# Edge stage of a graph attention layer: one exp into a PSUM bank, and the candidates' transposes moved ahead of the residual product

## What is computed

```python
h = (xn @ W).reshape(N, HEADS, HEAD_DIM)
a_src = jnp.einsum('nhd,hd->nh', h, att_src)
a_dst = jnp.einsum('nhd,hd->nh', h, att_dst)
e = jax.nn.leaky_relu(a_src[src] + a_dst[dst], NEG_SLOPE)
emax = jax.ops.segment_max(e, dst, num_segments=N)
ee = jnp.exp(e - emax[dst])
denom = jax.ops.segment_sum(ee, dst, num_segments=N)
agg = jax.ops.segment_sum(h[src] * (ee / denom[dst])[:, :, None], dst, num_segments=N)
out = agg.reshape(N, HEADS * HEAD_DIM) + xn @ W_res + bias
```

## Time and profile before

| | |
|---|---|
| median of 3 runs | 2565.8 us (2564.5 to 2571.7) |
| profiled execution | 2562.1 us |
| its span | 2560.9 us |
| TensorE busy, matmuls | 2062.0 us, 81% |
| VectorE busy | 1652.6 us, 65% |
| ScalarE busy | 1444.0 us, 56% |
| GpSimd busy | 1269.8 us, 50% |

### The profile page before, as it was taken

How to read it: one execution, slowest core, us unless ns; L and a number is a source line. 1 busy time by engine, 2 the same in 40 slices (tenths; PEclk the granted TensorE clock), 3 DMA queues, 4 the chain that set the end, 5 groups by cost and what they waited for, 6 DMA issues and landing times.

```text
span 2560.9 us, 51166 instructions
## 1 busy us (share of the span) xinstructions
PE 2062.0 (81%) x16814; PEld 1778.1 (69%) x16814; DVE 1652.6 (65%) x5168; ACT 1444.0 (56%) x3269; POOL 1269.8 (50%) x1155
## 2 busy tenths in 40 slices
PE   4637777777777777777776999997599999998995
PEld 3525555655555555555665888886599999998995
DVE  4518888888888888888997666664344444443442
ACT  2345555555555555555654666664456656565662
POOL 2167777777777777777740233333123223222221
PEclk8757777777877777777778999997799999999997
DMA  5565555655665565555542222211655254446534
GB/s 139 180 168 167 167 168 173 172 171 171 177 184 173 171 175 170 173 168 173 167 155 85 64 88 84 71 68 54 220 174 165 53 174 102 118 116 230 169 57 117
DMA packets 212241, 369.19 MB, mean 144 GB/s; under 512 B 43768, under 2 KB 147284, under 8 KB 203016
## 3 DMA queue, kind: packets, MB, share of 16 engines
q1 hardware_dynamic: 147560, 213.22, 24.6%
q0 software_dynamic: 63840, 151.61, 24.4%
q10 hardware_dynamic: 576, 1.09, 0.1%
HBM read 438.04 MB, written 101.93 MB: 211 GB/s over the span
## 4 chain that ended last, share of the span: by engine, by line
PE 54%; issue 12%; DVE 12%; ACT 10%; DMA 6%; POOL 3%; SPq 1%; DVEq 1%; ACTq 0%; POOLq 0%
PE bank L917 13%; PE bank L1082 8%; PE bank L1083 8%; PE bank L1084 8%; DVE edge_mem L983 4%; DMA expert_mem<-expert_rows 4%; PE bank L788 3%; ACT edge_mem L818 3%; PE bank L890 3%; PE bank L789 2%; PE bank L906 2%; DVE win_mem L1009 2%; DMA edge_mem<-in_x 1%; ACT piece_hi L710 1%; POOL expert_rows L1259 1%
## 5 line engine op out<-in xcount | busy, mean ns | idle before, releaser
L728 POOL DMA_INDIRECT edge_mem<-node_table,src_col x880 | 912.6, 1037 | 283.5 <-issue 265.2
L917 PE MATMUL bank<-edge_mem 128*128 128x264 f32 x1760 | 536.3, 467 | 15.7 <-DVE win_mem L1009 11.1
L1082 PE MATMUL bank<-expert_rounded 128*128 128x256 f32 x1792 | 517.2, 289 | 0.0
L1083 PE MATMUL bank<-expert_rounded 128*128 128x256 f32 x1792 | 512.4, 286 | 0.0
L1084 PE MATMUL bank<-expert_rounded 128*128 128x256 f32 x1792 | 512.2, 286 | 0.0
L917 PEld LDWEIGHTS bank<-edge_mem 128*128 128x128 f32 x1760 | 397.3, 234 | 133.2 <-issue 50.0
L1783 POOL DMA_INDIRECT sums<-expert_mem,slot_tok x112 | 190.0, 1697 | 546.1 <-DVE expert_mem L1721 459.7
L1770 ACT ACTIVATE expert_mem<-bank,par 128x256 f32<-128x256 f32 x448 | 228.6, 510 | 265.3 <-PE bank L1084 265.1
L1078 DVE TENSOR_TENSOR expert_rounded<-expert_mem,expert_rounded 128x512 fp32r<-128x512 f32 x280 | 193.9, 693 | 283.9 <-ACT expert_rounded L1770 218.5
L1082 PEld LDWEIGHTS bank<-expert_rounded 128*128 128x128 f32 x1792 | 349.9, 195 | 0.0
L1083 PEld LDWEIGHTS bank<-expert_rounded 128*128 128x128 f32 x1792 | 349.4, 195 | 0.0
(11 more groups left out here) (236 smaller groups left out, 3927.0 us busy)
## 6 DMA issues: line engine op xcount, KB each, us to landing
expert_rounded<-split_w SPq DMA_DIRECT2D x224, 1024.0 KB
split_w<-piece_hi SPq DMA_DIRECT2D x72, 256.0 KB
split_w<-piece_lo SPq DMA_DIRECT2D x72, 256.0 KB
piece_full<-in_L_ffn_W SPq DMA_DIRECT2D x64, 256.0 KB
expert_mem<-expert_rows SPq DMA_DIRECT2D x56, 265.0 KB, 3.5
edge_mem<-node_table,src_col POOLq DMA_INDIRECT x880
node_table<-win_mem SPq DMA_DIRECT2D x12, 544.0 KB, 3.8
xn_in<-turned SPq DMA_DIRECT2D x49, 128.0 KB
```

What stands on the lines that cost most here:

```text
L728: pool.indirect_dma_start(gath[g % NGB][:, t, :], None, node_table, bass.IndirectOffsetOnAxis(ap=src_col[:, k, t % 2:t % 2 + 1], axis=0)). ...
L917: ins = pe.matmul(bank[5 + at % 3][:, 0:AGG], onehot[g % 2][:, 2 * k + j, :], gath[g % NGB][:, 2 * k + j, 0:AGG], start=(j == 0), stop=(j ...
L1082: pe.matmul(out_ap, s_hi, m_lo, start=start, stop=False)
L1083: pe.matmul(out_ap, s_lo, m_hi, start=False, stop=False)
```

## The change

One SBUF tile `exponent` holds the scores of 16 tiles and, behind them, the factors' arguments of 8 steps. One exp turns both into a PSUM bank of its own (bank 2), from which `wgt` and `scale` are read; the exp of the factors alone and its semaphore go. The exp waits for the arguments, the scores, the messages and the adds of the round before. The maxima share bank 1 with the edge values, and the maxima's matmuls wait for the scores to be read. On TensorE the candidates' transposes come ahead of the residual product, on ScalarE the residual's copy comes behind the exp and the candidates' middle part.

```diff
--- before.py
+++ after.py
@@ -187,9 +187,8 @@
         rest = sb1("rest", [P, GS, 2 * HEADS])
         shift0 = sb1("shift0", [P, GS, HEADS])
         absent = sb1("absent", [P, GS])
-        scale = [sb1(f"scale{i}", [P, GS, HEADS]) for i in range(2)]
-        score = sb1("score", [P, GT, HEADS])
-        wgt = sb1("wgt", [P, GT, HEADS])
+        exponent = sb1("exponent", [P, GT + GS, HEADS])
+        score, scale_arg = exponent[:, 0:GT, :], exponent[:, GT:GT + GS, :]
         piece_full = [sb1(f"piece_full{i}", [P, PIECE]) for i in range(2)]
         piece_hi, piece_lo = ([sb1(f"piece_{n}{i}", [P, PIECE], F32R) for i in range(2)] for n in ("hi", "lo"))
         early.close()
@@ -314,7 +313,7 @@
         cand_turned, cand_high, cand_left, cand_middle, cand_split = (
             sem(n) for n in ("cand_turned", "cand_high", "cand_left", "cand_middle", "cand_split"))
         maxima_made, maxima_read = sem("maxima_made"), sem("maxima_read")
-        scale_taken, scale_ready, parts_ready = sem("scale_taken"), sem("scale_ready"), sem("parts_ready")
+        scale_taken, parts_ready = sem("scale_taken"), sem("parts_ready")
         edge_vals, scored, weights_ready, weighted = sem("edge_vals"), sem("scored"), sem("weights_ready"), sem("weighted")
         summed, added = sem("summed"), sem("added")
         edge_setup = sem("edge_setup")
@@ -656,7 +655,10 @@
                 ins.then_inc(last_ready, 1)
 
 
-        b_asrc, b_cand, b_ms, b_edge = bank[0], bank[0], bank[1], bank[2]
+        b_asrc, b_cand, b_edge = bank[0], bank[0], bank[1]
+        b_ms = bank[1][:, 16 * GT:16 * GT + 9 * GS]
+        b_exp = bank[2][:, 0:(GT + GS) * HEADS].rearrange("p (t h) -> p t h", h=HEADS)
+        wgt, scale = b_exp[:, 0:GT, :], b_exp[:, GT:GT + GS, :]
         b_res = bank[3][:, 0:D]
         assert NT <= NG
         n_small = 1 + KC + 3 + 3 * E
@@ -824,9 +826,6 @@
                     if n >= 1:
                         act.wait_ge(asrc_turned, n)
                     act.copy(asrc[:, :, :, :], gb[:, :, :, AGG:ROW].rearrange("p k j h -> p j k h")).then_inc(asrc_ready, 1)
-                if 0 <= g < NG:
-                    act.wait_ge(scale_taken, g + 1)
-                    act.activation(scale[g % 2][:, :, :], scale[g % 2][:, :, :], ACT.Exp).then_inc(scale_ready, 1)
                 if n < NG:
                     values = b_cand[:, EB:EB + P].rearrange("p (j k h) -> p j k h", j=2, k=GS)
                     if n >= 1:
@@ -835,16 +834,18 @@
                              last_col[:, n * GS:(n + 1) * GS, :].rearrange("p k j -> p j k").unsqueeze(3))
                     act.wait_ge(cand_turned, n + 1)
                     act.copy(cand[:, 0, :, :, 0:HEADS], values).then_inc(cand_high, 1)
-                if 0 <= g < NT:
-                    keep_residual(g)
                 if 0 <= g < NG:
+                    act.wait_ge(scale_taken, g + 1)
                     act.wait_ge(scored, g + 1)
                     if g >= 1:
                         act.wait_ge(weighted, NM * g)
-                    act.activation(wgt[:, :, :], score[:, :, :], ACT.Exp).then_inc(weights_ready, 1)
+                        act.wait_ge(added, GS * g)
+                    act.activation(b_exp, exponent[:, :, :], ACT.Exp).then_inc(weights_ready, 1)
                 if n < NG:
                     act.wait_ge(cand_left, n + 1)
                     act.copy(cand[:, 1, :, :, 0:HEADS], cand_rest[:, :, :, :]).then_inc(cand_middle, 1)
+                if 0 <= g < NT:
+                    keep_residual(g)
                 if 0 <= g < NG:
                     act.wait_ge(oh_ready, g + 1)
                     if g >= 2:
@@ -890,16 +891,19 @@
                             ins = pe.matmul(b_edge[:, t * 16:(t + 1) * 16], onehot_t[g % 2][:, t, :], parts[:, i, t // 2, :],
                                             start=(i == 0), stop=(i == 2))
                     ins.then_inc(edge_vals, 1)
-                if 0 <= g < NT:
-                    residual_product(g)
                 if n < NG:
                     pe.wait_ge(masked, n + 1)
                     for j in range(2):
                         ins = pe.transpose(b_cand[:, EB + j * 64:EB + (j + 1) * 64], seg_max[:, j * P:(j + 1) * P], ident[0:64, 0:64])
                     ins.then_inc(cand_turned, 1)
+                if 0 <= g < NT:
+                    residual_product(g)
+                if n < NG:
                     pe.wait_ge(cand_split, n + 1)
                     if n >= 1:
                         pe.wait_ge(maxima_read, n)
+                    if g >= 0:
+                        pe.wait_ge(scored, g + 1)
                     for k in range(GS):
                         for j in range(2):
                             for i in range(3):
@@ -962,9 +966,9 @@
                 yield
                 dve.wait_ge(dve_step, t)
                 t = step(dve.tensor_copy(parts[:, 0, :, :], nodeval[:, :, :]))
-                if g >= 2:
-                    dve.wait_ge(added, GS * (g - 2) + GS)
-                dve.tensor_tensor(scale[g % 2][:, :, :], shift0[:, :, :], nodeval[:, :, HEADS:2 * HEADS], ALU.subtract).then_inc(scale_taken, 1)
+                if g >= 1:
+                    dve.wait_ge(weights_ready, g)
+                dve.tensor_tensor(scale_arg, shift0[:, :, :], nodeval[:, :, HEADS:2 * HEADS], ALU.subtract).then_inc(scale_taken, 1)
                 yield
                 dve.wait_ge(dve_step, t)
                 t = step(dve.tensor_tensor(rest[:, :, :], nodeval[:, :, :], parts[:, 0, :, :], ALU.subtract))
@@ -999,10 +1003,10 @@
                         w = window(p, k)
                         acc = win[:, w, 0:AGG]
                         acc_h = acc.rearrange("p (h c) -> p h c", c=HC)
-                        dve.wait_ge(scale_ready, p + 1)
+                        dve.wait_ge(weights_ready, p + 1)
                         if at:
                             dve.wait_ge(added, at)
-                        t_scaled = step(dve.tensor_tensor(acc_h, acc_h, scale[p % 2][:, k, :].unsqueeze(2).to_broadcast([P, HEADS, HC]), ALU.mult))
+                        t_scaled = step(dve.tensor_tensor(acc_h, acc_h, scale[:, k, :].unsqueeze(2).to_broadcast([P, HEADS, HC]), ALU.mult))
                         next(small, None)
                         dve.wait_ge(dve_step, t_scaled)
                         dve.wait_ge(summed, at + 1)
```

## The result

The kernel after takes **2507.6 us** (median of 4 runs, 2506.4 to 2512.8) against 2568.15 of the kernel before, timed beside it (4 runs, 2564.5 to 2571.7): ratio 0.9773, 95% interval 0.9752 to 0.9794, 60 us faster.

What follows compares the result with a forecast made beforehand. It took a TensorE-ScalarE chain, VectorE's chain close beside it, and GpSimd's gathers as a floor to bound the kernel. 49 rounds x 1.28 us = 63 off 2562.1 gave 2499, stated as 2500 for the median; range 2478 to 2535.

Steps and rivals of the forecast that it cites:

- The candidates and the exponential: Edge round: candidates turned at T+1.17, exponential from T+2.23, L936 at T+6.37 instead of T+9.22; T is the round's opening scan.
- The sums and what is late next: Edge round: sums start at T+7.05 instead of T+8.33, then held by the widening copy behind the residual's copy.
- The size, 1.28 us a round: Sums start 1.28 us earlier in each of 49 rounds with a residual product, 63 us in all.
- The clock: TensorE's clock rose at T+12.4; with the idle before the maxima gone, an earlier rise would shorten residual product and first sums.
- Rival (b): Clock up: TensorE's chain falls below VectorE's and GpSimd's gather floor holds; 2482 us (2478 to 2490), chance 0.17.
- case (a): The forecast itself: 1.0 to 1.5 us gained per round, 2490 to 2514 us, chance 0.50.
- rival (c): Clock low as long as now, or first adds held behind late sums: 0.85 us per round, 2520 us, chance 0.20.
- PSUM at no cost: VectorE's message products and scalings read weights and factors from PSUM with no change in their time.
- Rival (e): Slower: VectorE reads PSUM with zero step at half rate, 4.5 us more per round, 2780 us, chance 0.05.
- VectorE's spare: Edge round: VectorE's chain ends at T+20.0 against TensorE's 20.8, so it has 0.8 us to spare.
- rival (d): Gathers stay held because VectorE's instruction, not its second input's place, is the cause: 2558 us, no change, chance 0.08.
- the cap of 4 us: If GpSimd's gathers stay as they are, the last one limits all savings ahead of it to 4 us.

Runs made afterwards that it cites:

- loads_copy: Kernel after with SyncE loads replacing gathers, and ScalarE's residual copy put back ahead of the exponential: 2589.1 us, against 2521.8 without that move.
- loads_widen: Kernel after with SyncE loads replacing gathers, and ScalarE's widening copy put ahead of the residual's copy: 2474.0 us, against 2521.8 without that move.
- six_gathers: Kernel after with 10 of 16 tiles per group loaded by SyncE, six gathered; exponential into PSUM in even groups, SBUF in odd: 2545.3 us.
- order_only: Kernel after with the exponential's results in an SBUF tile instead of PSUM: 3446.8 us, against 3445.9 for the kernel before on that chip.
- widen_first: Kernel after with ScalarE's residual copy moved behind the widening copy, gathers kept: ratio 0.9995 to the kernel before (3445.9 us) on that chip.

## Why the prediction came out right, step by step

**The candidates and the exponential**: L897 at T+1.17 to 1.19, the exponential at T+2.05 to 2.49, L940 at T+6.18 to 6.55 over the 49 rounds: as foretold to 0.26 us. loads_copy shows that TensorE's order alone isn't enough; ScalarE's alone was not run.

**The sums and what is late next**: in rounds whose residual product runs at the low clock they start at T+7.1, 0.10 us behind L853, as foretold. loads_widen shows that it was L853.

**The size, 1.28 us a round, is the term that was mis-sized**; it came out at 1.18. I had read it from one common round and given it to all 49, those at the higher clock too. By the length of the residual product:

| residual product | rounds before | round | sums from T | rounds after | round | sums from T |
|---|---|---|---|---|---|---|
| over 3.1 us | 30 | 22.15 | 8.17 | 31 | 20.72 | 7.09 |
| 2 to 3.1 us | 10 | 21.63 | 7.65 | 18 | 20.45 | 6.45 |
| under 2 us | 9 | 20.81 | 6.56 | 0 | | |

In nine rounds before, the residual product took 1.7 us, so that there was less to take away; and after the change no such round is left. In the long rounds too the sums start 1.08 us earlier and not 1.28, since the round that I read had them at T+8.33 and their mean was T+8.17. The mean residual product is 3.02 us instead of 2.82. The change moved it from T+0.93 to T+1.52, and in the rounds from 760 to 1030 us of after the clock falls between T+0.5 and T+2.2: less of it is done before the fall (2.81 us of it lie at the low clock in the mean, 2.38 before). The sums start 0.92 us earlier in the mean (T+7.77 to T+6.85), and from there to the next scan it takes 13.76 us instead of 14.03; of these 0.27 us, 0.16 are the sums themselves (9.98 to 9.82). I had foreseen no gain there. So 1.28 was 0.36 too much for the start of the sums and 0.27 too little behind it; that the two nearly cancel, and the round came within 0.10 us, is luck. That the banks are freed earlier because VectorE now waits for sums and not they for it is argued, not shown.

The last step of the sum has a slip of its own: 2565.8 - 63 is 2503 and not 2500. Measured were 2507.6.

**The clock**: the thought that an earlier rise, once the idle ahead of the maxima was gone, would shorten the round has nothing for it. The round of 787.02 in windows (us, busy of each engine, granted clock, DMA share, GB/s):

```profile
787.02:788.90 1.88, 1.83 (x49) 1.64 (x46) 1.74 (x6) 0.27 (x1) 1.27 (x3) 0.97 0.87 216
788.90:797.60 8.70, 7.77 (x63) 5.48 (x62) 7.08 (x19) 6.64 (x18) 6.59 (x7) 0.50 0.93 313
797.60:807.37 9.77, 7.43 (x50) 6.09 (x50) 9.14 (x38) 5.67 (x9) 7.57 (x8) 0.93 0.45 121
```

It rises at 799.0, T+12.0, where it rose at T+12.4 in the round read before. That pair proves little, since the rise lies between T+9.2 and T+13.9 in the rounds of before and between T+9.1 and T+13.2 in those of after. Its mean is T+11.8 before and T+11.3 after, so it did come 0.45 us earlier, but the time at the low clock did not shrink by that: 10.47 us a round before, 10.38 after (513 and 508 us in the 49). So the 57.8 us saved are nearly all time at the high clock, and the mean granted clock went from 0.76 to 0.75. Rival (b) needed more time at the high clock and rounds held by the gathers, and has neither (2 of 55 asrc copies wait for gathers); the forecast's own case (a), 1.0 to 1.5 us a round, is what came. The mechanism of rival (c), low for as long as now, is what the trace shows; its time is not: the round is 1.18 us shorter and not 0.85, so that the 0.4 us that I put on it are too many. What the clock costs by itself no run shows.

**PSUM at no cost** was right: L1009 takes 427 ns with the operand in PSUM where L1005 took 435, L987 776 ns in the mean of its forms against 781 for L983, and six_gathers has the pairs side by side. Rival (e) falls (the first L987 takes 1.25 us, not 2). The Trainium skill (Perfetto Trace Analysis, section Optimizing Scalar/DVE Operations) has VectorE's access to PSUM about 65 ns dearer than that to SBUF, which I had made 0.98 us a round, an estimate. The traces do not confirm it for this form: 4 to 6 ns less instead of 65 more.

**VectorE's spare**, put at 0.8 us a round, was there: its adds wait 59.2 us for the sums, 1.2 us a round, and in loads_widen another 0.98 us came off the round with VectorE's program unchanged.

**The gathers**: that the change would set them free was right in cause and size (838.0 us against 840), so rival (d) falls. My counts of them in the kernel before had left some out: of all that begin inside an L1005 164 of 191 are long, inside an L983 113 of 142, inside an L1009 0 of 108, and most of the others begin in the last 0.15 us of the instruction; the reading stands. Whether setting them free was needed is not shown. It added no time to what the orders gave: without gathers the change brings 1.17 us a round, with them 1.18. But the cap of 4 us for gathers that stay held, on which the step rests, was never tested. For that order_only would have to run where gathers and TensorE go side by side. From the rows the argument stands: a group of held gathers takes 21.47 us and the round is now 20.62. The shape fits too: GpSimd's lead over the last asrc copy grew from 8.8 to 19.9 us.

**The five rounds without a residual** are as before: 18.83 us against 18.87 for the first of them.

## What to carry to other kernels

When two engines each keep a fixed order, an instruction that many wait for must be moved ahead on both: with TensorE's order alone, ScalarE's put the wait back, and here that cost 10 to 14 us where both together gained 53. Size such a gain from every kind of round that the stage has, at the high clock as well as the low, not from the commonest. And when a new first wait is named by the profile, look also at what ended just before on the third engine: moving that one (the widening copy, which ended 0.1 us ahead of the sums and which the profile did not name for them) was worth another 48 us in the form without gathers.

## What the runs showed of the hardware that I had not expected

- On the chips of the experiments, beside GpSimd's gathers, TensorE gets its instructions 0.5 to 1.5 us apart, and VectorE and ScalarE go on long after it has done what they wait for (842.1 against 829.4, 12.7 us). An identical program, the kernel before, takes 3446 us instead of 2568 there; the round of widen_first is 37.5 us. The late supply begins some 3 us (six_gathers) to 5 us (widen_first) after the first gather and ends 3 to 3.6 us after the last. With the rows loaded by SyncE, as many bytes through another queue, it is gone (3449 to 2575 us). Whether the issue of the gathers or their transfers do it is open. The Trainium skill (SBUF — State Buffer, section Who interferes with whom) says that TensorE and ScalarE never wait on anyone; for the ports of SBUF that may be, but here their work stands behind the gathers, and whether the instructions or the signals come late is not shown. Why it is so on the five chips of the experiments, and was not in the runs of the result, stays open too.
- A gather that begins beside an instruction of VectorE with both operands in SBUF takes up to 1.85 us instead of 0.95; one beside an instruction of the same size with an operand in PSUM is never longer (0 of 101).
- Less idle on TensorE gave no more time at the high clock: 114.9 us of idle ahead of the maxima were gone in 49 rounds (36.9 us ahead of the sums came instead), and the time at the low clock stayed (513 us before, 508 after). What the change took away was time at the high clock.
